# A linear-attention block with adaptive layer norms and a look-up feed-forward network: reciprocals spread by DMA, loads reordered, and second-norm rows turned by transposing DMAs

## The reference, cut to what matters

```python
h = _layernorm(x) * (1 + ca) + sa
x = x + ga * _attn(h)          # out = (elu(q)+1) @ kv / (z + eps), then @ o_w.T + o_b
h = _layernorm(x) * (1 + cb) + sb
x = x + gb * _ffn(h)           # w = lut[idx]; down(silu(gate(h)) * up(h))
```

## Time and profile before

| | |
|---|---|
| median of three runs | 1146.49 us |
| the profiled execution | 1147.93 us |
| its span | 1145.7 us |
| TensorE matmul busy | 1105.9 us (97%) |
| VectorE busy | 867.5 us (76%) |
| ScalarE busy | 516.8 us (45%) |
| GpSimd busy | 370.6 us (32%) |
| DMA, share of 16 engines' span (hardware queue) | 41.9% |
| granted TensorE clock, mean | 0.992 |

### The profile page before, as it was taken

The page is one execution under the profiler, slowest core; times in us unless marked ns, Lnnn a source line. Parts: engine busy times, 40 slices in busy tenths (PEclk is TensorE's granted clock), DMA queues, the critical chain, the costliest instruction groups (busy, mean ns, idle before and its releaser), DMA issues.

```text
span 1145.7 us, 19116 instructions
## 1 busy us (share of the span) xinstructions
PE 1105.9 (97%) x7508; PEld 610.2 (53%) x7534; DVE 867.5 (76%) x1251; ACT 516.8 (45%) x877; POOL 370.6 (32%) x331
## 2 busy tenths in 40 slices
PE   4899999999999799999999999999999999999998
PEld 2344444544444344444544444444444468888887
DVE  4688988776779568898766987956743968887884
ACT  4667787777726233242421423324224742333231
POOL 1000100002115255474722735726434222222222
PEclk9899999999999899999999999999999999999999
DMA  7930231123112843333322414323242466888872
GB/s 270 324 123 20 89 111 67 46 74 111 37 39 80 276 148 102 138 111 117 127 106 94 157 72 152 113 110 117 76 155 82 158 224 218 257 278 280 272 253 101
DMA packets 115736, 162.79 MB, mean 142 GB/s; under 512 B 7520, under 2 KB 70496, under 8 KB 111552
## 3 DMA queue, kind: packets, MB, share of 16 engines
q1 hardware_dynamic: 115648, 161.58, 41.9%
HBM read 92.88 MB, written 68.68 MB: 141 GB/s over the span
## 4 chain that ended last, share of the span: by engine, by line
PE 84%; DVE 7%; issue 4%; ACT 3%; POOL 1%; DMA 1%; SPq 0%; POOLq 0%; DVEq 0%; ACTq 0%
PE bank L1437 20%; PE bank L1439 20%; PE bank L1438 20%; PE bank L1753 5%; PE bank L1754 5%; PE bank L1755 5%; PE bank L1445 2%; DVE look_buf L1116 2%; PE bank L1589 1%; DMA w_ffn<-in_wmod 1%; DVE w_ffn L1116 1%; PE bank L1507 1%; PE bank L1571 1%; PE bank L1550 1%; PE bank L1757 1%
## 5 line engine op out<-in xcount | busy, mean ns | idle before, releaser
L631 POOL TENSOR_TENSOR shared<-hid_f,shared 128x512 f16<-128x512 f32 (+1 forms) x88 | 117.6, 1336 | 279.2 <-ACT shared L845 279.1
L1437 PE MATMUL bank<-h,w_ffn 128*128 128x512 f16 (+1 forms) x528 | 200.4, 379 | 0.3 <-POOL h L610 0.3
L1438 PE MATMUL bank<-h,w_ffn 128*128 128x512 f16 (+1 forms) x528 | 200.1, 379 | 0.0
L1439 PE MATMUL bank<-h,w_ffn 128*128 128x512 f16 (+1 forms) x528 | 200.1, 379 | 0.0
L845 ACT ACTIVATE shared<-hid_f 128x512 f16<-128x512 f32 (+1 forms) x88 | 55.5, 630 | 249.4 <-DVE hid_f L1281 249.2
L1281 DVE SCALAR_TENSOR_TENSOR hid_f<-bank,sc,shared 128x512 f32<-128x512 f32 (+1 forms) x88 | 65.6, 746 | 100.1 <-PE bank L1439 40.8
L1437 PE MATMUL bank<-arena,h 128*128 128x512 f16 x256 | 98.8, 386 | 5.7 <-issue 2.7
L837 ACT ACTIVATE shared<-bank,sc 128x512 f32<-128x512 f32 (+1 forms) x88 | 60.1, 683 | 96.8 <-PE bank L1439 96.4
L1113 DVE TENSOR_SCALAR look_buf<-look_buf,tab_x,tab 128x512 uint32<-128x512 uint32 x147 | 101.0, 711 | 0.6
L1438 PE MATMUL bank<-arena,h 128*128 128x512 f16 x256 | 98.3, 384 | 0.0
L1439 PE MATMUL bank<-arena,h 128*128 128x512 f16 x256 | 98.3, 384 | 0.0
(11 more groups left out here) (287 smaller groups left out, 2606.2 us busy)
## 6 DMA issues: line engine op xcount, KB each, us to landing
full_dram<-hid_f SPq DMA_DIRECT2D x80, 256.0 KB, 2.0
hid_dram<-shared SPq DMA_DIRECT2D x80, 256.0 KB, 2.0
w_ffn<-full_dram SPq DMA_DIRECT2D x16, 1280.0 KB, 9.9
xg<-in_x SPq DMA_DIRECT2D x16, 1024.0 KB, 7.0
qp_dram<-qp SPq DMA_DIRECT2D x8, 1024.0 KB, 4.9
x_dram<-xg SPq DMA_DIRECT2D x8, 1024.0 KB, 4.1
xg<-x_dram SPq DMA_DIRECT2D x8, 1024.0 KB, 7.2
qn<-hid_dram SPq DMA_DIRECT2D x24, 320.0 KB, 4.0
```

Source lines behind the costliest of these rows:

```text
L631: pool.tensor_tensor(hid[0:m, e % HIDS, :, 1], whole, hid[0:m, e % HIDS, :, 0], ALU.subtract).then_inc(hid_done, 1)
L1437: pe.matmul(dst, a_hi, b_hi, start=first, stop=False)
L1438: pe.matmul(dst, a_hi, b_lo, start=False, stop=False)
L1439: last = pe.matmul(dst, a_lo, b_hi, start=False, stop=end)
```

## The change

1. The turning of the second norm. For groups 3 to 7 (`TURNED` = 3) `xn_b`, `t_piece`, `h_b` and `h_lo_b` go. The scale and shift vectors are written to DRAM once (in stage A, group 2) and read back, once a batch, as rows copied to all 128 partitions (`mod2_load`, into the two buffers `h_f`). Then, tile by tile: ScalarE normalises (`xn2_full`), GpSimd multiplies by the scale row (`xn2_scale`), VectorE adds the shift row (`xn2_shift`), ScalarE rounds to the high part (`xn2_hi`), GpSimd subtracts for the low part (`xn2_lo`), and SyncE turns high and low parts of the tile, 128 x 1024 of 16 bits, with one transposing DMA from SBUF to SBUF (`h2_turn`). Tiles 0 and 1 are turned at SyncE's step 7, tiles 2 and 3 at its step 9. There are two buffers of each kind. The first gate matmul of a group waits for all four turns. In the diff below the four pieces behind the loads on SyncE are, in this order, of GpSimd, ScalarE, VectorE and TensorE.
2. The spreading of the reciprocals. For groups 4 to 7 (`SPREAD` = 4) `z_spread` and the second half of `rec` go. `z_store` writes the reciprocals to DRAM at SyncE's step 5 (4 stores), `z_load` reads them back copied to 32 partitions for each head (8 loads at step 6 and 8 at step 8), and `qn_full` multiplies with that SBUF buffer in place. `qn_full`, `qn_hi`, `qn_lo` of chunks 2 and 3 move to steps 8 and 9, those of chunks 0 and 1 by one step.
3. Order. In s0 the query load, the first `x1_store` and the output-weight load go to steps 1, 2 and 3, and the eleven index loads are spread from (s0, step 5) to (s1, step 2). From s2 on `x_next` goes from step 5 to 8 and `q_next` from 8 to 10; GpSimd's `xob` goes from step 9 to 10.

```diff
+DOWN_LOADS = {(0, 5): (0, 1), (0, 6): (2, 3), (0, 7): (4, 5), (0, 8): (6, 7), (1, 0): (8,), (1, 1): (9,), (1, 2): (10,)}
+SPREAD = 4
+TURNED = 3
...
+        mod2_row = h_f
+        xn2_f = part(arena, 2 * tile_w, F32, 2, HID)
+        xn2_parts = part(arena, 2 * tile_w + 2 * HID, F16, 2, 2 * HID)
...
+                if g == 2:
+                    sp.wait_ge(h2_ready, 1)
+                    for w in range(2):
+                        for b in range(BATCHES):
+                            sp.dma_start(mod2_dram[w, b].rearrange("(k p) -> p k", p=P), modm[:, 2 + w, :, b],
+                                         allow_slow_non_contiguous=True).then_inc(rows2_out, 16)
...
+            def mod2_load(b):
+                sp.wait_ge(rows2_out, 16 * 2 * BATCHES)
+                if b == 0:
+                    sp.wait_ge(h2_done, 4 * TURNED + 4)
+                else:
+                    sp.wait_ge(x_shifted, 4 * (PER_BATCH - TURNED))
+                for w in range(2):
+                    sp.dma_start(mod2_row[:, w], mod2_dram[w, b].partition_broadcast(P)).then_inc(rows2_in, 16)
+            def h2_turn(n, t):
+                sp.wait_ge(x_low, 4 * (n - TURNED) + t + 1)
+                if t == 0:
+                    sp.wait_ge(up_done, SLOT[(n - H2S, FC - 1)] + 1)
+                turned = h2[n % H2S].rearrange("p s k n -> p (s k) n")[:, :, t * P:(t + 1) * P]
+                sp.dma_start_transpose(turned, xn2_parts[:, t % 2]).then_inc(h2_in[t % 2], 16)
+            def z_store(n):
+                sp.wait_ge(rec_done, n + 1)
+                for c in range(KC):
+                    heads = z_dram[n][c * P // HEAD:(c + 1) * P // HEAD].rearrange("i (r k) -> r i k", r=COPIES)
+                    sp.dma_start(heads, z_cols[c * HEAD:(c + 1) * HEAD]).then_inc(z_out, 16)
+            def z_load(n, c):
+                if c == 0:
+                    sp.wait_ge(z_out, 16 * KC * (n - SPREAD + 1))
+                sp.wait_ge(qn_done, 4 * n + c + 3)
+                for i in range(P // HEAD):
+                    sp.dma_start(qn_f[i * HEAD:(i + 1) * HEAD, c % 2], z_dram[n][c * P // HEAD + i].partition_broadcast(HEAD)).then_inc(z_in[c % 2], 16)
...
-                store, nxt = (6, 7) if s == 0 else (3, 5)
+                store, nxt = (6, 7) if s == 0 else (3, 5) if n < TURNED else (3, 8)
...
+                        if n >= TURNED:
+                            if i == 0 and n == TURNED:
+                                mod2_load(0)
+                            if i == 1 and n == PER_BATCH:
+                                mod2_load(1)
+                            if i in (7, 9):
+                                h2_turn(n, i - 7)
+                                h2_turn(n, i - 6)
                         if i == nxt:
                             x_next(n, n % 2)
-                        if i == 8 and n + 2 < GROUPS:
+                        if n + 1 >= SPREAD and n + 1 < GROUPS:
+                            if i == 5:
+                                z_store(n + 1)
+                            elif i in (6, 8):
+                                z_load(n + 1, i - 6)
+                                z_load(n + 1, i - 5)
+                        if i == (8 if s < 2 else 10) and n + 2 < GROUPS:
...
+            def xn2_scale(n, t):
+                pool.wait_ge(xf_done, 4 * (n - TURNED) + t + 1)
+                pool.tensor_tensor(xn2_f[:, t % 2], xn2_f[:, t % 2], mod2_row[:, 0], ALU.mult).then_inc(x_scaled, 1)
+            def xn2_lo(n, t):
+                pool.wait_ge(x_high, 4 * (n - TURNED) + t + 1)
+                pool.tensor_tensor(xn2_parts[:, t % 2, HID:2 * HID], xn2_f[:, t % 2], xn2_parts[:, t % 2, 0:HID], ALU.subtract).then_inc(x_low, 1)
...
+                    if n >= TURNED:
+                        before = {}
+                        after = {3: [lambda: norm(n, stats2_done, ve2_done, rstd2_done, nmr2_done)],
+                                 4: [lambda: xn2_scale(n, 0), lambda: xn2_scale(n, 1)], 5: [lambda: xn2_lo(n, 0), lambda: xn2_lo(n, 1)],
+                                 6: [lambda: xn2_scale(n, 2), lambda: xn2_scale(n, 3)], 8: [lambda: xn2_lo(n, 2), lambda: xn2_lo(n, 3)]}
...
+            def xn2_full(n, t):
+                if k >= 2:
+                    act.wait_ge(x_low, k - 1)
+                act.activation(xn2_f[:, t % 2], xg[:, n % 2, t], ACT.Identity, bias=nmr[:, t:t + 1], scale=rstd[:, t:t + 1]).then_inc(xf_done, 1)
+            def xn2_hi(n, t):
+                act.wait_ge(x_shifted, k + 1)
+                if k >= 2:
+                    act.wait_ge(h2_in[t % 2], 16 * (k // 2))
+                act.activation(xn2_parts[:, t % 2, 0:HID], xn2_f[:, t % 2], ACT.Copy).then_inc(x_high, 1)
...
+                        after = {4: [lambda: xn2_full(n, 0), lambda: xn2_full(n, 1)], 5: [lambda: xn2_hi(n, 0), lambda: xn2_hi(n, 1)],
+                                 6: [lambda: xn2_full(n, 2), lambda: xn2_full(n, 3)], 7: [lambda: xn2_hi(n, 2), lambda: xn2_hi(n, 3)]}
...
+                if n >= SPREAD:
+                    dve.reciprocal(z_cols[:], z_cols[:]).then_inc(rec_done, 1)
+                    return
+            def xn2_shift(n, t):
+                dve.wait_ge(x_scaled, 4 * (n - TURNED) + t + 1)
+                dve.tensor_tensor(xn2_f[:, t % 2], xn2_f[:, t % 2], mod2_row[:, 1], ALU.add).then_inc(x_shifted, 1)
+                            after.setdefault(5 + t // 2 * 2, []).append(lambda t=t: xn2_shift(n, t))
...
-                    if j == 0 and w == 0:
+                    if j == 0 and w == 0 and g < TURNED:
                         pe.wait_ge(h2_done, 4 * g + 4 + k + 1)
+                    elif j == 0 and w == 0 and k == 0:
+                        for i in range(2):
+                            pe.wait_ge(h2_in[i], 32 * (g - TURNED + 1))
```

More of the change, by code:

```diff
@@ L459, in hid_load @@
                 sp.dma_start(left_last[i][0:TAIL], hid_dram[g][0:TAIL, FC - 1, t:t + 2]).then_inc(hid_in[i], 16)
-            x1_store(0, 0)
             for s in range(GROUPS):
                 n = s + 1
-                store, nxt = (6, 7) if s == 0 else (3, 5)
+                store, nxt = (6, 7) if s == 0 else (3, 5) if n < TURNED else (3, 8)
                 for i, (g, j) in enumerate(STAGES[s]):
                     e, m = SLOT[(g, j)], rows_of(j)
-                    if s == 0 and i == 3:
-                        x_next(0, 0)
-                    if s == 0 and i == 4:
-                        sp.wait_ge(x2T_done, 8)
-                        sp.wait_ge(qn_f_done, 8)
-                        for jd in range(FC):
-                            md = rows_of(jd)
-                            sp.dma_start(down_idx[0:md, jd], downT[jd * P:jd * P + md, :]).then_inc(idx_in[4], 16)
+                    if s == 0:
+                        if i == 1:
+                            sp.wait_ge(qp_out, 16 * 8 + 16)
+                            sp.dma_start(flat(qp[:]), qp_dram[2]).then_inc(q_in, 16)
+                        elif i == 2:
+                            x1_store(0, 0)
+                        elif i == 3:
+                            sp.dma_start(owt[1], chunked(owT)).then_inc(ow_in[1], 16)
+                        elif i == 4:
+                            x_next(0, 0)
+                        elif i == 5:
+                            sp.wait_ge(x2T_done, 8)
+                            sp.wait_ge(qn_f_done, 8)
+                    for jd in DOWN_LOADS.get((s, i), ()):
+                        md = rows_of(jd)
+                        sp.dma_start(down_idx[0:md, jd], downT[jd * P:jd * P + md, :]).then_inc(idx_in[4], 16)
                     if s < GROUPS - 1:
@@ L606, in xn_b @@
                                        ALU.mult, ALU.add).then_inc(xn2_done, 1)
+            def xn2_scale(n, t):
+                if t == 0 and n in (TURNED, PER_BATCH):
+                    wait_apart(pool, rows2_in, 32 * (n // PER_BATCH + 1))
+                pool.wait_ge(xf_done, 4 * (n - TURNED) + t + 1)
[3 more added lines that the diff above has]
+                pool.tensor_tensor(xn2_parts[:, t % 2, HID:2 * HID], xn2_f[:, t % 2], xn2_parts[:, t % 2, 0:HID], ALU.subtract).then_inc(x_low, 1)
             def h_lo_b(n, c):
@@ L898, in stage_b @@
                         before[4] = [lambda: den(n + 1)]
-                        before[6] = [lambda: qn_hi(n + 1, 0), lambda: qn_hi(n + 1, 1), lambda: h_b(n, 0)]
-                        before[7] = [lambda: qn_hi(n + 1, 2), lambda: qn_hi(n + 1, 3), lambda: h_b(n, 2)]
+                        first, second = (7, 9) if n + 1 >= SPREAD else (6, 7)
+                        before[first] = [lambda: qn_hi(n + 1, 0), lambda: qn_hi(n + 1, 1)] + before.get(first, [])
+                        before[second] = [lambda: qn_hi(n + 1, 2), lambda: qn_hi(n + 1, 3)] + before.get(second, [])
                 for i, (g, j) in enumerate(STAGES[s]):
@@ L1366, in stage_b @@
                         after[4] = [lambda: rec(n + 1)]
-                        after[5] = [lambda: qn_full(n + 1, 0), lambda: qn_full(n + 1, 1)]
```

(7 more changed lines are left out.)

47 lines of the change are left out of this document (35 added, 12 removed).

## The result

The median of four runs is 1154.91 us (1152.24 to 1155.45), that of the kernel before on the same chip 1146.06 us (1145.07 to 1148.01): a ratio of 1.007, 95% interval 1.005 to 1.0091. The forecast was 1132.9, so the sign is wrong and the time lies above the range. The profiled execution took 1152.24 us (span 1150.1), the fastest of its four, against 1147.93 (span 1145.7): the two traces differ by 4.4 us of the 8.9 that the medians show. They explain these 4.4. What made the other runs of this kernel longer no trace shows. One stretch can be compared in all traces, from TensorE's last matmul ahead of the gap in s0 to its first of the last phase: 555.9 us before (379.71 to 935.63), 560.8 after (378.44 to 939.23).

What follows compares the result with a forecast made beforehand. TensorE was taken as the bound, VectorE nearly a second one in stages' second halves. Gains of 8.7 + 9.2 + 6.9 = 24.8 us less 11.2 of stalls leave 13.6: 1132.9 us against the 1146.49 median, range 1121 to 1150.

Steps and rivals of the forecast that it cites:

- Terms 1 and 2: TensorE, s2 to s6: removed transposes save 8.7 us and removed spreading matmuls 9.2 us, 17.9 us in all.
- Term 3: Load order in s0: TensorE's gap falls from 6.73 to 1.95 us and 2.15 us of slow clock goes, gain 6.9 us.
- Rival B: The queue of s0 stays the brake, a store still late, the load-order gain 0: 1139.8 us; chance 0.12.
- T: What the transposing DMA takes after a stage's last tile is ready: taken as 5 us, bounds 2.0 and 12.2.
- Rival C: Transposing DMA itself slows groups 4 to 7; from T = 8.4 on stalls eat the whole gain; chance 0.16.
- Term 4: Turned rows late at stage ends: stalls of 5.2 us twice and 0.4 us twice, 11.2 us in all.
- In s5 and s6, with a lag near 0.2: VectorE hardly late at the ends of s5 and s6: stall T - 4.6 if positive, 0.4 us each.
- s2 has 15 steps and none: Stage s2, with 15 steps, was to have no stall from late turned rows.
- the reciprocals of chunks 2 and 3 queue behind it: SyncE's 1 MB load at step 8 delays these loads, costing VectorE some us after its product, inside its margin.
- +1.0 us for VectorE: VectorE slowed beside GpSimd's new scalings in a stage's second half: 1.0 us taken, between 0 and 1.9.
- The test that I named: VectorE's products of step 8 in s3 and s4 should start some 5 us behind the matmuls.

Runs made afterwards that it cites:

- no_look: Changed kernel with the 1 MB load of x at step 10 and the look-ups from unit 24 on left out: 1123.73 us, ratio 0.9807.
- spread_only: Changed kernel with the rows still turned on TensorE, keeping the new order and the reciprocals by DMA: 1133.96 us, ratio 0.9882.
- order_only: Changed kernel without turned rows and without the spread by DMA, only the new order: 1140.32 us, ratio 0.9938.
- xnext_late: Changed kernel with the 1 MB load of x moved from step 8 to step 10, behind the reciprocals' loads: 1146.71 us, ratio 1.0005.
- split: Changed kernel, 1 MB load at step 10, look-ups moved: none in steps 5 to 7 of s3 to s6 or 5 to 8 of s2: 1128.99 us.
- turn_6: Changed kernel with only groups 6 and 7 turned by DMA, the 1 MB load at step 10 and look-up units 30 to 32 moved: 1132.49 us.
- turn_7: Changed kernel with only group 7 (stage s6) turned by DMA, look-ups and loads as in the change: 1131.56 us, ratio 0.9867.

## Why the prediction was wrong, point by point

**Terms 1 and 2, 17.9 us: right.** no_look, where TensorE meets no stall at a stage start, shows the full gain within 2 us; spread_only shows the second term, with 4 us of new gaps beside it.

**Term 3, 6.9 us: right.** 1.95 us was forecast for the gap, and it is 1.95 to 1.97 in all twelve kernels with the new order; the ledger of order_only gives 7.0. Rival B fell with it.

**T, 5 us: right.** 3.5 us to landing, 4.0 to 5.2 until TensorE starts. Rival C had the sign, but not the mechanism: it needed T above 8.4.

**Term 4, 11.2 us: this is the step that failed.** Its mechanism, the turned rows late by VectorE's lag plus the chain plus T, is what the trace shows for s3 and s4. That the sizes agree there (5.8 and 5.4 us for 5.2) is in part luck: the lag was 6.9 and 7.9 us for 5, the chain behind it 4.9 for 5.55 and T 4.3 and 4.0 for 5, and in s4 a gap of 1.0 us in step 9 gave the rows time. Three of its entries and one omission were wrong:

- *"In s5 and s6, with a lag near 0.2"*: the lag at step 8 of s5 is 5.4 us, and the stall 5.1 for 0.4. I had derived 5 us for the stages with three look-up units and let the stage with two off, for its VectorE has idle time: 27.01 of 34.90 us in the earlier trace rows, and 25.05 of 35.00 afterwards. A share over half a stage was the wrong measure. At step 7, 6.5 us went by between the end of its matmuls and its product, in short waits and in operations at 1.4 us. For s6 (0.4 forecast, 0 found) it was right.
- *"s2 has 15 steps and none"*: 4.0 us. That "the reciprocals of chunks 2 and 3 queue behind it, which costs VectorE some us in step 8 after its product, inside its margin" was named and priced at nothing. The wait was 6.0 us and the work in the list behind it came on top; xnext_late, which moves only that load, brought this gap to 1.5 us and took 3.8 us off the stretch.
- *"+1.0 us for VectorE"* beside GpSimd. Of the 29 us by which VectorE's busy time grew, the twenty shifts are 15.4 (0.81 us each, 0.7 forecast) and the spread tables' products took 3.5 away; about 17 us are instructions of before that became longer. Paired one by one in the two traces, the same instructions are 1.1 us longer in s2, 1.3 in s3, 4.8 in s4, 5.7 in s5 and 2.0 in s6, and the products of the queries some 1.2 more in each of s2 to s5. I had taken 1.0 for a half stage.
- *Not in the sum:* the lower clock behind each stall, 8.9 us. The earlier trace rows had shown 2.15 us for one gap of 6.7. I counted its end as a gain in term 3 and forgot it for gaps that I forecast myself.

So stalls of 11.2 became 21.3 (the four gaps, 20.3, and the one of 1.0 inside s4), and 8.9 came on top: 24.8 - 30.2 = -5.4 us, where the spans say -4.4 (the ledger, which also counts 0.5 us of lower clock elsewhere before, gives -4.9). The trace does not reach the median, which is 2.7 us further.

**The test that I named** (VectorE's products of step 8 in s3 and s4 some 5 us behind) came out at 6.9 us in s3 and 7.9 in s4. It stood for s5 as well, where I had not expected it. A sum with one margin for each stage, 10.34 us against lag plus 5.55 plus T, would have shown that T of 5 leaves no margin at all in any stage: each microsecond of lag above -0.2 is paid in full, and with the clock more than once. The miss in s5, 4.7 us and the slow matmuls behind it, hung on a number that I had read from an average.

What stays open: how much of VectorE's slow-down is due to GpSimd's new product form and how much to more overlap of the two (of line 1234, 23 operations lay wholly beside GpSimd after and 21 before, but at 1.37 us for 1.20; no run changes the form alone); whether the shifts without the look-ups, or the look-ups without the shifts, would do; the gaps of 1.9 to 2.5 us that split has at 509, 570 and 810 us; and turn_6 against turn_7.

## What to carry to other kernels

When work leaves the bound engine for a chain over several in-order lists, write the deadline at the chain's end and the margin of every stage with the lag of the busiest helper in it, taken from the steps themselves and not from busy shares; then keep background work out of just those steps (16.5 us here, between two tables with the same units in each stage). Small loads that somebody waits for go ahead of a 1 MB load on the same queue (3.8 us in the traces here, 8 by the medians), and a gap in the bound engine is priced with the slow matmuls behind it. Where a change of several parts loses, run its parts: two of the three here gain 1.2% without the third.
